# Triangular solve on one engine, one convolution tap and the update keys on others, and the diagonal blocks turned in one piece, in a gated delta-rule layer with experts

## The chip, the cores and the metric

One core of a Trainium2 chip runs the whole kernel as one program. It has five engines that run side by side, each with its own queue of instructions in a fixed order: PE (matrix products), DVE (vector), ACT (activations and copies), POOL (general elementwise work, indirect DMAs) and SP (DMA issues). They are kept in order by semaphores. The metric is device time in microseconds of one execution, median over runs.

## The reference

2048 tokens of width 256 pass two residual blocks in fp32. The first is a gated delta-rule layer with 8 key heads and 16 value heads of width 64; the second, 32 experts with 4 per token and a shared one.

```
qkv  = silu(causal_conv4(x @ W_qkv.T))          # depthwise, 4 taps, 2048 channels
q, k = l2norm(q) / 8, l2norm(k)                 # 8 heads, each used by two value heads
for t:                                          # per value head, state S is 64 x 64
    S     = S * exp(g_t)
    delta = (v_t - k_t @ S) * beta_t
    S     = S + outer(k_t, delta)
    o_t   = q_t @ S
y = rmsnorm(o) * norm_weight * silu(x @ W_z.T);   x = x + y @ W_out.T
x = x + moe(rmsnorm(layernorm(x))) + ...        # router, top 4, expert products, shared expert
```

## The kernel before, in words

The recurrence runs in chunks of C = 64 tokens (32 of them, `n`). Two chunks make a block of 128 tokens (`b`, 16), four make a pair (`p`, 8 pairs). Within a chunk the recurrence is a unit lower triangular system of 64 x 64 for each of the 16 heads, which is solved in advance for a whole pair: 4 chunks x 16 heads, split in diagonal blocks of H = 32 x 32, lie across the 128 partitions as 32 systems side by side.

One list, `SCHEDULE`, sets the order of all work. Each step has a due time in the tables `FRONT` (once for each pair), `CHAIN` (each chunk), `TAIL` (each block) and `GATE` (each pair); the list is sorted by due time, and every engine walks it and takes its own part of each step, in that order. The work of pair p+1's front stands between the chunks of pair p and the tails of its blocks. No step overtakes another in an engine's queue.

The steps that matter here, with their engines:

- `proj`, `mul`, `tap`, `silu`: the convolution, in 8 steps `s_` of two channel tiles `i`. PE projects 256 tokens and their halo into one of three PSUM banks in turn; ACT (line 600) copies it times the first tap to `ca` (two buffers, by `f % 2`); DVE (line 785) adds three taps from PSUM to it, 128x256 each; ACT (line 613) takes silu to `kqn` (steps 0 to 3, queries and keys) or `vraw` (4 to 7, values), and for queries and keys the squares (line 618). `ss`, `ssq`, `rpow` (POOL, line 477, a power) make the norms. A bank is free again after its last tap.
- `kt`, `kn`, `kb`, `ke`, `kk`, `nd`, `scan`, `nt`: keys by token (`ktok`) and normalised, decays by a scan (line 807), and the products (lines 818 and 819) to `ntx`, the triangular matrices, and `at`.
- `lx` (line 827): DVE turns the four diagonal blocks, 32 partitions each, to `nl`.
- `el`, j = 0 to 30: the forward elimination, a product with broadcast operands to a scratch tile (line 424) and a sum onto `tl` (line 427). Step j works on 31 - j rows; POOL takes columns 0 to 5, DVE columns 6 to j, each with a chain of its own. `xt` (lines 839, 840) turns the result; `pm`, `pe`, `tm`, `tc` make the lower left block of the inverse.
- For each chunk: `kqs` (POOL, line 519, two scalings), `ks`, `r`, `qs`, `sd` (POOL, line 527, scales the state), `u` (PE), then `up` (DVE, line 844), which scales u row by row by the decays to the end of the chunk, negated and times beta, into `rr`; `ue` (ACT, line 655) copies u to `us`; `ku` (PE, line 1147) multiplies keys and `rr`, two value heads of one key head at a time; `su` (DVE, line 849) adds to the state; `au`, `oe` give the output (ACT, line 661).
- For each block: `osq` (ACT, line 666), `nin`, `npow`, `yn` (DVE, line 868), `yt`, `yg` (DVE, line 874), `op` (PE, line 1187), `x2` (DVE, line 882), `xn`, `hh` and the router with its top 4 (`ex` on ACT, line 684; `tk`; `slot`, ending at line 931), `send` (POOL, line 546, four indirect DMAs). `z` and `zs` (PE, line 1171; ACT, line 671, silu) make the gates.

After the last pair come the experts, which the change doesn't touch.

## Time and profile before

| | us |
|---|---|
| median of 3 runs | 1326.2 (1325.64 to 1330.1) |
| the profiled execution | 1323.6 |
| its span | 1321.7 |
| busy: PE / DVE / ACT / POOL | 989.4 / 823.2 / 455.4 / 618.0 |
| mean granted clock of PE | 0.832 of full speed |

The profile is one execution; its span leaves out 1.9 us around the program. In a timeline each line begins with the start in us from the span's start and the duration in us; then engine, source line, operation, output and inputs, shapes, and the number of instructions. In brackets stands how long the engine was idle before and what ended that. Neighbouring instructions of an engine overlap a little, so that the distance from start to start is shorter than a duration. In a view by lines the columns behind the count are busy us, mean ns of one instruction and idle us before.

### The profile page before, as it was taken

The page shows a single profiled execution, that of the slowest core. Times are in us where ns is not written, and L with a number is a line of the kernel's source. Part 1 is how long each engine was busy: PE and PEld are TensorE (multiplying, and loading weights), DVE is VectorE, ACT ScalarE, POOL GpSimd, SP SyncE. Part 2 cuts the span into 40 slices and gives each one's busy share as a digit, 9 for nine tenths or more (in the row PEclk, how much of TensorE's full clock was granted, in tenths as well). Part 3 has the DMA queues.
Part 4 walks back from the last instruction along what each step waited for, and adds up shares of the span by engine and source line. Part 5 has one row for each costly group of instructions (what it writes and reads, how often), then busy time and mean ns, then how long its engine had stood idle before and what let it go on. Part 6 is the DMA issues. An engine that isn't in the chain of part 4 may idle for free.

```text
span 1321.7 us, 32155 instructions
## 1 busy us (share of the span) xinstructions
PE 989.4 (75%) x12359; PEld 810.8 (61%) x12359; DVE 823.2 (62%) x1947; ACT 455.4 (34%) x890; POOL 618.0 (47%) x907
## 2 busy tenths in 40 slices
PE   0673687787688879868787986878685799998950
PEld 0662675676577667657666765766675457776730
DVE  5169469569848956984895698489544243333335
ACT  1331422542253244225324422532422124444420
POOL 2036248447545744764484476448343013554530
PEclk9776789698778969877896987789588699999985
DMA  5270232505253360535336152533685922444437
GB/s 206 83 190 18 70 85 52 163 22 153 71 152 104 103 173 23 153 66 157 103 98 173 29 153 66 157 97 83 185 282 186 358 69 81 126 134 123 118 124 222
DMA packets 182356, 165.61 MB, mean 125 GB/s; under 512 B 75699, under 2 KB 174908, under 8 KB 181312
## 3 DMA queue, kind: packets, MB, share of 16 engines
q1 hardware_dynamic: 172272, 144.60, 38.9%
q0 software_dynamic: 7632, 16.87, 4.0%
q8 instruction: 102, 1.67, 0.5%
q10 hardware_dynamic: 2304, 2.10, 0.5%
q14 instruction: 46, 0.38, 0.1%
HBM read 66.03 MB, written 101.55 MB: 127 GB/s over the span
## 4 chain that ended last, share of the span: by engine, by line
PE 44%; DVE 34%; issue 9%; DMA 6%; ACT 4%; SPq 1%; POOL 1%; DVEq 0%; POOLq 0%; ACTq 0%
DVE arena L785 9%; PE ps L1039 5%; PE ps L1187 5%; PE ps L1249 5%; DVE arena L427 5%; DVE arena L424 4%; PE ps L1171 3%; PE ps L1102 3%; PE ps L1048 2%; PE ps L1092 2%; PE ps L1111 2%; PE ps L1272 2%; DMA out<-work 2%; PE ps L1156 2%; DMA work<-htd 2%
## 5 line engine op out<-in xcount | busy, mean ns | idle before, releaser
L785 DVE SCALAR_TENSOR_TENSOR arena<-ps,cw,arena 128x256 f32<-128x256 f32 x384 | 156.1, 475 | 84.2 <-ACT arena L600 83.1
L1039 PE MATMUL ps<-work,arena 128*128 128x259 f32 x512 | 162.6, 454 | 26.9 <-DVE arena L785 24.6
L557 POOL DMA_INDIRECT picked<-work x95 | 93.4, 983 | 111.4 <-DVE work L974 66.1
L1039 PEld LDWEIGHTS ps<-work,arena 128*128 128x128 f32 x512 | 107.4, 222 | 55.7 <-DVE arena L785 29.4
L600 ACT ACTIVATE arena<-ps,cw 128x256 f32<-128x256 f32 x128 | 60.2, 470 | 198.9 <-PE ps L1039 198.4
L546 POOL DMA_INDIRECT slotted<-hr,slots x64 | 63.3, 989 | 138.7 <-DVE slots L931 124.0
L964 DVE TENSOR_TENSOR work<-work,ps 128x128 f32<-128x128 f32 (+1 forms) x111 | 34.0, 307 | 140.6 <-ACT work L700 116.1
L477 POOL TENSOR_TENSOR rn<-rin,mhalf 128x16 f32<-128x16 f32 x16 | 46.5, 2906 | 153.7 <-DVE rin L791 153.7
L1249 PE MATMUL ps<-arena,work 128*128 x380 | 100.7, 387 | 7.4 <-issue 6.2
L427 POOL TENSOR_TENSOR arena<-arena 128x60 f32<-128x60 f32 (+29 forms) x248 | 92.1, 372 | 19.4
L424 POOL TENSOR_TENSOR arena<-arena 128x60 f32<-128x60 f32 (+29 forms) x248 | 89.4, 360 | 24.1 <-DVE arena L827 7.8
L1187 PE MATMUL ps<-work 128*128 128x256 f32 x256 | 73.9, 453 | 25.6 <-DVE work L874 25.6
L1171 PE MATMUL ps<-work 128*128 128x256 f32 x256 | 74.3, 440 | 18.8 <-DVE cnt L926 18.1
L427 DVE TENSOR_TENSOR arena<-arena 128x25 f32<-128x25 f32 (+12 forms) x200 | 81.2, 406 | 6.9
L1187 PEld LDWEIGHTS ps<-work 128*128 128x128 f32 x256 | 59.2, 235 | 40.4 <-DVE work L874 28.9
L613 ACT ACTIVATE arena<-arena 128x512 f32<-128x512 f32 x64 | 40.2, 629 | 123.2 <-DVE arena L785 123.2
L424 DVE TENSOR_TENSOR arena<-arena 128x25 f32<-128x25 f32 (+12 forms) x200 | 76.4, 382 | 4.3
L519 POOL TENSOR_TENSOR work<-arena,work 128x512 f32<-128x512 f32 x64 | 75.6, 1200 | 6.2 <-DMA work<-tab 6.0
L1249 PEld LDWEIGHTS ps<-arena,work 128*128 128x128 f32 x380 | 64.7, 190 | 18.9 <-issue 13.9
L700 ACT ACTIVATE work<-ps 128x128 f32<-128x128 f32 (+1 forms) x111 | 32.5, 292 | 120.8 <-PE ps L1240 56.9
L1171 PEld LDWEIGHTS ps<-work 128*128 128x128 f32 x256 | 52.3, 215 | 31.0 <-DVE cnt L926 18.9
L477 POOL TENSOR_TENSOR small<-small,mhalf 128x1 f32<-128x1 f32 x32 | 22.8, 713 | 97.9 <-DVE small L886 51.8
(221 smaller groups left out, 2234.7 us busy)
## 6 DMA issues: line engine op xcount, KB each, us to landing
slotted<-blank SPq DMA_DIRECT2D x17, 4128.0 KB
arena<-in_w SPq DMA_DIRECT2D x2, 6528.0 KB, 20.1
work<-slotted SPq DMA_DIRECT2D x95, 129.0 KB
arena<-tab SPq DMA_DIRECT2D x64, 128.0 KB, 3.5
work<-tab SPq DMA_DIRECT2D x64, 128.0 KB
...
```

Source lines behind the costliest of these rows:

```text
L424: e.tensor_tensor(t, nl[:, j + 1:H, j:j + 1].broadcast_to([P, rows, cols]), tl[:, j:j + 1, lo:hi].broadcast_to([P, rows, cols]), ALU.mult) ...
L427: e.tensor_tensor(tl[:, j + 1:H, lo:hi], tl[:, j + 1:H, lo:hi], t, ALU.add).then_inc(S[name], 1)
L477: g.tensor_tensor(out_, in_, mhalf[:, 0:in_.shape[1]], ALU.pow).then_inc(S[name], 1)
L519: g.tensor_tensor(kqs[:, n % 2, kind, :, :].rearrange("p (kt r) t -> p kt r t", r=2), kqn[:, p % 2, kind, :, lo:lo + C].unsqueeze(2).broad ...
L546: g.indirect_dma_start(out=slotted, out_offset=bass.IndirectOffsetOnAxis(ap=slots[:, k:k + 1], axis=0), in_=hr[:, k, :], in_offset=None).t ...
L557: g.indirect_dma_start(out=picked, out_offset=bass.IndirectOffsetOnAxis(ap=to, axis=0), in_=yrow[:, j % SLOTS, :], in_offset=None, bounds_ ...
L600: a.activation(ca[:, f % 2, i, :], bank_of("proj", p, s_, i)[:, 0:W2], ACT.Copy, scale=cw[:, u, 0:1]).then_inc(S["mul_out"], 1)
L785: v.scalar_tensor_tensor(out=acc_, in0=bank_of("proj", p, s_, i)[:, k:k + W2], scalar=cw[:, u, k:k + 1], in1=acc_, op0=ALU.mult, op1=ALU.a ...
L1039: ins = mm(to[:, 0:WX], wqkv[:, k, m:m + P], xt2[:, p % 3, k, :], start=k == 0, stop=k == KD - 1)
L1171: ins = mm(W3[:, W2 * j:W2 * j + W2], wz[:, d, m:m + P], xt2[:, p % 3, d, TAPS - 1:TAPS - 1 + W2], start=d == 0, stop=d == KD - 1)
L1187: ins = mm(W3[:, 0:DIM], ygt[:, u, :], wo[:, u, :], start=u == 0, stop=u == UT - 1)
L1249: ins = mm(up_[:, 0:2 * I], ht[:, j % 2, k, :], arena[:, bass.ds(at_ + 2 * I * k, 2 * I)], start=k == 0, stop=k == KD - 1)
```

## The change

Four edits and their new places in the order.

1. All columns of the elimination go to DVE, in one chain (62 instructions a pair instead of 50, on more elements); POOL's 62 small ones go.
2. The second tap is an ACT copy (scaled) into the place where silu's result will stand; DVE adds two taps; a new step `sum` on POOL adds the two 128x512 tiles; silu waits for it and its due time moves from 6.5 to 7.5.
3. `up` goes. A new POOL step `ktb` scales the keys instead, for each value head, ahead of the chunk; `ue` waits for u alone, and `ku` takes `ktb` and `us` in products of 64 columns, twice as many.
4. A new ACT step `lg` gathers the diagonal blocks with three copies into `xr`, and `lx` is one DVE transpose.

```diff
-SPLIT = 6
-ER = 2 * (H - 1 - SPLIT)
...
-         (24.5, "rpow", 1), (35, "lx"), (68, "xt"), (69, "tl"), (71, "pm"), (74, "pe"), (76, "tm"), (79, "tc")]
+         (24.5, "rpow", 1), (34.5, "lg"), (35, "lx"), (68, "xt"), (69, "tl"), (71, "pm"), (74, "pe"), (76, "tm"), (79, "tc")]
-          for t, what, *more in ((0, ("proj",), 0), (0.5, ("mul",), 0), (2, ("proj",), 1), (2.5, ("mul",), 1), (3.5, ("tap",)), (6.5, ("silu",)))]
-CHAIN = [(-14, "kqs"), (-13.9, "ebload"), (-4, "v"), (0, "ks"), (0.5, "qs"), (3, "r"), (4, "sd"), (4.5, "u"), (6.5, "up"), (7, "ue"),
+          for t, what, *more in ((0, ("proj",), 0), (0.5, ("mul",), 0), (2, ("proj",), 1), (2.5, ("mul",), 1), (3.5, ("tap",)), (6, ("sum",)), (7.5, ("silu",)))]
+CHAIN = [(-14, "kqs"), (-13.9, "ebload"), (-4, "v"), (0, "ks"), (0.5, "qs"), (3, "r"), (4, "sd"), (4.5, "u"), (-8, "ktb"), (6.5, "ue"),
...
     if name == "proj":
-        return [("tap", 6 * (8 * p + ix[0]) + 5 + ix[1])]
+        return [("tap", 4 * (8 * p + ix[0]) + 3 + ix[1])]
...
+        def conv_to(p, s_):
+            if s_ < 4:
+                return kqn[:, p % 2, s_ // 2, 2 * (s_ % 2):2 * (s_ % 2) + 2, :]
+            return vraw[:, p % 2, 2 * (s_ - 4):2 * (s_ - 3), :]
...
-                if name == "el":
...
-                    eliminate(pool, g, p, j, 0, min(SPLIT, j + 1), solve_tmp, "el_pool", EL * p + 2 * j)
+                if name == "sum":
+                    pool.wait_ge(S["tap"], 4 * f + 4)
+                    pool.wait_ge(S["mul_out"], 4 * f + 4)
+                    g.tensor_tensor(ca[:, f % 2, :, :], ca[:, f % 2, :, :], conv_to(p, s_), ALU.add).then_inc(S["sum_out"], 1)
+                if name == "ktb":
+                    pool.wait_ge(S["kn_out"], n // 2 + 1)
+                    pool.wait_ge(S["ndb_out"], 1)
+                    wait(pool, S["ku_mm"], n)
+                    g.tensor_tensor(ktb.rearrange("p (kt r) d -> p kt r d", r=2),
+                                    ktok[:, n // 2 % 4, n % 2, :, :].unsqueeze(2).broadcast_to([P, KT, 2, DH]),
+                                    ndb[:, n, :].rearrange("p (kt r) -> p kt r", r=2).unsqueeze(3).broadcast_to([P, KT, 2, DH]),
+                                    ALU.mult).then_inc(S["ktb_out"], 1)
...
+                    a.activation(ca[:, f % 2, i, :], from_[:, 0:W2], ACT.Copy, scale=cw[:, u, 0:1]).then_inc(S["mul_out"], 1)
+                    a.activation(conv_to(p, s_)[:, i, :], from_[:, 1:1 + W2], ACT.Copy, scale=cw[:, u, 1:2]).then_inc(S["mul_out"], 1)
                 if name == "silu":
-                    act.wait_ge(S["tap"], 6 * f + 6)
+                    act.wait_ge(S["sum_out"], f + 1)
+                if name == "lg":
+                    act.wait_ge(S["at_out"], 4 * p + 4)
+                    wait(act, S["pm_mm"], p)
+                    a.activation(xr, ntx[:, 0:H, :], ACT.Copy).then_inc(S["lg_out"], 1)
+                    act.wait_ge(S["lg_out"], 3 * p + 1)
+                    for e in range(2):
+                        own = slice(C * e + H, C * e + C)
+                        a.activation(xr[own], ntx[own, H:C, :], ACT.Copy).then_inc(S["lg_out"], 1)
                 if name == "r":
-                    wait(act, S["ku_mm"], n)
+                    wait(act, S["u_mm"], n)
                 if name == "ue":
-                    act.wait_ge(S["up_out"], n + 1)
+                    act.wait_ge(S["u_mm"], n + 1)
...
+            def eliminate(p, j):
+                rows, cols = H - 1 - j, j + 1
...
+                v.tensor_tensor(t, nl[:, j + 1:H, j:j + 1].broadcast_to([P, rows, cols]),
+                                tl[:, j:j + 1, 0:cols].broadcast_to([P, rows, cols]), ALU.mult).then_inc(S["el"], 1)
+                dve.wait_ge(S["el"], step + 1)
+                v.tensor_tensor(tl[:, j + 1:H, 0:cols], tl[:, j + 1:H, 0:cols], t, ALU.add).then_inc(S["el"], 1)
                 if name == "tap":
-                    dve.wait_ge(S["mul_out"], 2 * f + 2)
-                    for k in range(1, TAPS):
+                    for k in range(2, TAPS):
                         for i in range(2):
-                            if k > 1:
-                                dve.wait_ge(S["tap"], 6 * f + 2 * k - 3 + i)
+                            if k == 2:
+                                dve.wait_ge(S["mul_out"], 4 * f + 2 * i + 2)
+                            else:
+                                dve.wait_ge(S["tap"], 4 * f + i + 1)
                 if name == "lx":
-                    for q in range(4):
-                        rows, own = slice(H * q, H * q + H), slice(H * (q % 2), H * (q % 2) + H)
-                        v.transpose(nl[rows], ntx[rows, own, :]).then_inc(S["lx_out"], 1)
+                    dve.wait_ge(S["lg_out"], 3 * p + 3)
+                    v.transpose(nl, xr).then_inc(S["lx_out"], 1)
-                if name == "up":
-                    dve.wait_ge(S["u_mm"], n + 1)
-                    v.tensor_tensor(rr, by_head(UR), ndb[:, n, :].unsqueeze(2).broadcast_to([P, KR, DH]), ALU.mult).then_inc(S["up_out"], 1)
...
-                    pe.wait_ge(S["up_out"], n + 1)
+                    pe.wait_ge(S["ue_out"], n + 1)
+                    pe.wait_ge(S["ktb_out"], n + 1)
-                    for kt in range(KT):
+                    for h in range(KR):
                         for hp in range(2):
-                            ins = mm(KU[half(hp), P * kt:P * kt + P], ktok[half(hp), n // 2 % 4, n % 2, kt, :],
-                                     rr[half(hp), 2 * kt:2 * kt + 2, :].rearrange("p r d -> p (r d)"), start=True, stop=True)
+                            ins = mm(KU[half(hp), DH * h:DH * h + DH], ktb[half(hp), h, :], us[half(hp), h, :], start=True, stop=True)
```

By the new due times ACT's order in a pair reads (s for silu, m for the copies of a step and tile): m0,0 m0,1 r m1,0 m1,1 ue s0 m2,0 m2,1 s1 m3,0 oe m3,1 s2 s3 ke ke ht r ex ue lg oe osq zs m4,0 zs m4,1 zs zs r s4 ... ht r ex s7 ue pe oe osq tc. POOL's reads: sd sum0 kqs sum1 ktb rpow sum2 nd lnp sum3 nd rmp nd rpow nd sd kqs ktb send npow sum4 sd kqs sum5 ktb lnp sum6 rmp sd sum7 tl kqs ktb send npow. PE's is as before.

## Rows read from the trace of the kernel before

**Rows 1.** Stretches: us, busy PE, PEld, DVE, ACT, POOL, clock, DMA, GB/s

```profile
470.20:585.90 115.70, 92.97 (x1380) 78.44 (x1380) 86.32 (x205) 43.99 (x70) 65.02 (x96) 0.82 0.43 111
935.40:1015.40 80.00, 65.93 (x1048) 57.35 (x1048) 35.39 (x104) 27.60 (x41) 26.97 (x24) 0.78 0.72 224
1015.40:1321.70 306.30, 227.21 (x1057) 167.74 (x1056) 119.14 (x328) 96.57 (x326) 105.28 (x106) 0.88 0.51 157
```

**Rows 2.** Timelines of DVE, ACT and PE around the turns, pair 4

```profile
538.27 0.69 DVE L819 TENSOR_TENSOR arena<-ps,arena 128x512 f32<-128x512 f32 x1
...
539.92 5.04 DVE L827 STREAM_TRANSPOSE arena<-arena 32x1024 f32<-32x1024 f32 x4
...
548.49 2.44 DVE L785 SCALAR_TENSOR_TENSOR arena<-ps,cw,arena 128x256 f32<-128x256 f32 x6 [1.70 <-ACT arena L600]
...
535.94 1.28 ACT L671 ACT_TABLE_LOAD   x1
542.93 0.60 ACT L671 ACTIVATE work<-ps 128x512 f32<-128x512 f32 x1 [5.71 <-PE ps L1171]
...
545.07 2.00 PE L1171 MATMUL ps<-work 128*128 128x256 f32 x8
```

**Rows 3.** Timeline of DVE while it solves, pair 4

```profile
571.61 0.41 DVE L882 TENSOR_TENSOR row<-xin,ps 128x256 f32<-128x256 f32 x1
...
572.97 2.45 DVE L785 SCALAR_TENSOR_TENSOR arena<-ps,cw,arena 128x256 f32<-128x256 f32 x6
...
576.75 0.31 DVE L424 TENSOR_TENSOR arena<-arena 128x144 f32<-128x144 f32 x1
577.10 0.31 DVE L427 TENSOR_TENSOR arena<-arena 128x144 f32<-128x144 f32 x1
...
584.49 0.17 DVE L424 TENSOR_TENSOR arena<-arena 128x25 f32<-128x25 f32 x1
584.69 0.18 DVE L427 TENSOR_TENSOR arena<-arena 128x25 f32<-128x25 f32 x1
```

**Rows 4.** By lines, whole span: count, busy, mean ns, idle before

```profile
L519 POOL TENSOR_TENSOR work<-arena,work 128x512 f32<-128x512 f32 x64 | 75.6, 1200 | 6.2 <-DMA work<-tab 6.0
...
L600 ACT ACTIVATE arena<-ps,cw 128x256 f32<-128x256 f32 x128 | 60.2, 470 | 198.9 <-PE ps L1039 198.4
...
L844 DVE TENSOR_TENSOR work<-ps,ndb 128x512 f32<-128x512 f32 x32 | 21.8, 681 | 9.1 <-PE ps L1138 9.1
...
L666 ACT ACTIVATE work<-work 128x1024 f32<-128x1024 f32 x16 | 16.9, 1058 | 0.5
...
L839 DVE STREAM_TRANSPOSE arena<-arena 128x1024 f32<-128x1024 f32 x8 | 10.0, 1245 | 0.8
```

**Rows 5.** Timelines of DVE and POOL where both read SBUF

```profile
562.37 1.08 DVE L424 TENSOR_TENSOR arena<-arena 128x144 f32<-128x144 f32 x1
...
562.14 2.26 POOL L519 TENSOR_TENSOR work<-arena,work 128x512 f32<-128x512 f32 x2
...
551.62 1.23 DVE L868 TENSOR_TENSOR work<-work,nrm 128x1024 f32<-128x1024 f32 x1
...
551.63 1.53 POOL L424 TENSOR_TENSOR arena<-arena 128x135 f32<-128x135 f32 x1
...
933.10 1.08 DVE L424 TENSOR_TENSOR arena<-arena 128x25 f32<-128x25 f32 x1
```

**Rows 6.** Timelines of PE and POOL in the first steps, pair 4

```profile
503.67 2.03 PE L1048 MATMUL ps<-parind,arena 128*64 128x1 f32 x64 [0.66 <-ACT arena L618]
...
506.53 2.90 POOL L477 TENSOR_TENSOR rn<-rin,mhalf 128x16 f32<-128x16 f32 x1 [9.32 <-DVE rin L791]
```

**Rows 7.** Timeline of ACT behind the solve, pair 4

```profile
476.52 1.08 ACT L628 ACTIVATE arena<-ps 128x512 f32<-128x512 f32 x2 [2.32 <-PE ps L1092]
```

**Rows 8.** Timeline of DVE in pair 0, first and last of its solve

```profile
105.66 2.44 DVE L785 SCALAR_TENSOR_TENSOR arena<-ps,cw,arena 128x256 f32<-128x256 f32 x6
...
135.35 1.25 DVE L839 STREAM_TRANSPOSE arena<-arena 128x1024 f32<-128x1024 f32 x1
```

More of the change, by code:

```diff
@@ L184, in gated_delta_moe @@
         vraw = carve(2, UT, W2)
+        ktb = carve(KR, DH)
         parts = ((0, early), (early, EV))
@@ L416, in _ @@
                 sp.wait_ge(s_o[k], 16 * (NB // 2))
-        def eliminate(engine, e, p, j, lo, hi, scratch, name, step):
-            rows, cols = H - 1 - j, hi - lo
-            t = scratch[:, 0:rows * cols].rearrange("p (i k) -> p i k", i=rows)
-            if step % (2 * (H - 1 - lo)):
-                engine.wait_ge(S[name], step)
-            e.tensor_tensor(t, nl[:, j + 1:H, j:j + 1].broadcast_to([P, rows, cols]),
-                            tl[:, j:j + 1, lo:hi].broadcast_to([P, rows, cols]), ALU.mult).then_inc(S[name], 1)
-            engine.wait_ge(S[name], step + 1)
-            e.tensor_tensor(tl[:, j + 1:H, lo:hi], tl[:, j + 1:H, lo:hi], t, ALU.add).then_inc(S[name], 1)
         @block.gpsimd
@@ L616, in stage @@
                         wait(act, S["pm_mm"], p)
-                        wait(act, S["lx_out"], 4 * p)
+                        wait(act, S["lg_out"], 3 * p)
                         a.activation(sq[:, 2 * s_:2 * s_ + 2, :], dst, ACT.Square).then_inc(S["sqr_out"], 1)
+                if name == "lg":
+                    p, = ix
+                    act.wait_ge(S["at_out"], 4 * p + 4)
[5 more added lines that the diff above has]
+                        a.activation(xr[own], ntx[own, H:C, :], ACT.Copy).then_inc(S["lg_out"], 1)
                 if name == "ke":
@@ L773, in _ @@
             psum_, pinv, wsum, winv = (small[:, 15, k:k + 1] for k in range(4))
+            def eliminate(p, j):
+                rows, cols = H - 1 - j, j + 1
+                step = EL * p + 2 * j
+                t = solve_tmp[:, 0:rows * cols].rearrange("p (i k) -> p i k", i=rows)
+                if j == 0:
+                    dve.wait_ge(S["lx_out"], p + 1)
+                else:
+                    dve.wait_ge(S["el"], step)
+                v.tensor_tensor(t, nl[:, j + 1:H, j:j + 1].broadcast_to([P, rows, cols]),
+                                tl[:, j:j + 1, 0:cols].broadcast_to([P, rows, cols]), ALU.mult).then_inc(S["el"], 1)
+                dve.wait_ge(S["el"], step + 1)
+                v.tensor_tensor(tl[:, j + 1:H, 0:cols], tl[:, j + 1:H, 0:cols], t, ALU.add).then_inc(S["el"], 1)
             def stage(name, *ix):
@@ L797, in stage @@
                     dve.wait_ge(S["rn_out"], 2 * p + 1)
-                    wait(dve, S["ku_mm"], 2 * (b - 3))
+                    wait(dve, S["ktb_out"], 2 * (b - 3))
                     v.tensor_tensor(ktok[:, b % 4, :, :, :].rearrange("p e kt d -> p (e kt) d"),
```

43 lines of the change are left out of this document (17 added, 26 removed).

## The prediction

> **What bounds the kernel now.** I read the table of stretches first. Seven of the eight pairs repeat: the one from 470.2 to 585.9 takes 115.7 us, with DVE busy 86.3 us and PE 93.0, and the six others like it 115.8 to 117.4 [rows 1]. The span is a sum of such periods, with a head, an 80 us tail of the last chunks and 306 us of experts behind them [rows 1], which the change touches little or not at all. No engine is full over it, so I cut one pair (pair 4, 470.2 to 585.9) by what DVE waits for, in its own order of time. Four parts come out.
> A, 472.5 to 495.6: after the two turns of the solved blocks PE, ACT and the chunk's work run in line; DVE has long gaps.
> B, 495.6 to 516.7: four steps "projection, ACT copy, taps, silu"; PE and ACT set the pace.
> C and D, 516.7 to 550.9: scans and decay products on DVE until 539.0, then the four turns of the diagonal blocks (5.04 us), while ACT gates z; the taps of step 4 start at 548.49 after an idle gap for ACT's copies [rows 2].
> E, 550.85 (end of those taps) to 584.87 (end of the last elimination step, in front of the turns): DVE is back to back, 34.0 us, with no wait worth naming [rows 3]. It is the one part that DVE sets alone, and all of DVE's eliminations (from j = 6) lie in it.
> So DVE's share of a period, three quarters, says little: an instruction taken from DVE is worth its time in E and nearly nothing in A and B.
>
> **Solve on DVE, alone.** When POOL is idle a step on 25 elements takes 0.17 us and the next starts 0.20 later; one on 144 takes 0.31 and the next starts 0.35 later [rows 3]; two more of the kind give 0.34 and 0.33 for 144 and 133. That makes 0.17 us plus 1.18 ns per element from start to start. After the change step j works on (31-j)(j+1) elements, twice. Over j = 3 to 30 that is 56 instructions and 10,556 elements: 9.5 + 12.5 = 22.0 us. Steps 0 to 2 (6 instructions, 1.5 us) fall into the gap ahead of the taps of step 4, which DVE has today and keeps; if the gap were gone they would cost 1.5 us.
>
> **Taps, keys, turns.** Six taps of a step take 2.44 us, 0.39 from start to start [rows 2, 3]; four take 1.6. E holds three steps: 4.8 us instead of 7.2. The update scaling (L844, 0.68 us, 0.60 start to start [rows 4]) leaves DVE: one of the four in a pair lies in E, one in C, two in A or B beside waits. The rest of E stays: the normalisation 1.55, two gatings 1.2, the state 0.6, the residual and its statistics 1.35 (571.61 to 572.97 [rows 3]), the layer norm 0.65, the row h 0.8: 6.15 us. Uncontended E is thus 22.0 + 4.8 + 6.15 = 32.95 us, 1.1 less than now.
>
> **The lock.** DVE and POOL don't run at the same time when both read two SBUF tensors. While POOL's two key scalings ran (562.14, 2.26 us together), two DVE steps of 144 elements took 1.08 each (the first stands in the rows), against 0.31 alone: 0.77 lost apiece. The other way round, POOL's 135-element step that began with DVE's normalisation at 551.62 took 1.53 us [rows 5]. Taps read PSUM and one SBUF tensor and keep their 2.44 us beside POOL's steps [rows 2]. Today this costs E about 4.6 us: its 50 steps (5,850 elements) are worth 15.4 us alone by the formula and fill 34.0 - 7.2 - 0.6 - 6.15 = 20.0. The change takes POOL's small steps away, which pays that back, but puts large instructions in their place. In E stand four sums, one key scaling for the update (ktb), and, as before, two of kqs and one or two of sd, all 128x512 with two SBUF inputs, 1.04 us by themselves and 1.20 in the mean [rows 4]. A sum is released by the end of the taps, just when DVE goes back to the solve. Eight such instructions at 0.77 are 6.2 us. The bounds: 3 us, if half of them meet PSUM instructions or gaps, and 8.3 us, if each holds DVE for its 1.04. I take 0.77, the row that shows exactly this meeting. E becomes 32.95 + 6.2 = 39.1 us, 5.0 more than now.
> The Trainium skill (SBUF — State Buffer, section "Who interferes with whom") says that a Vector instruction with two SBUF inputs contends with a GpSimd instruction that reads SBUF and that the loser blocks for the whole of it. The rows above agree on who contends with whom; they show 0.77 us where the whole instruction would be 1.04, and by the page E would be 41.2 us instead of 39.1.
>
> **Turns and ACT (D).** Before: 5.04 us of turns from 539.92 [rows 2]. After: ACT gathers first, one copy of 128x1024 and two of 32x1024, each 1.06 us (as L666), in series some 3.2 us with the wait between them, then one turn of 1.25 (as L839) [rows 4]. The solve can begin 1.4 us sooner. But lg sits in ACT's queue ahead of oe, osq and the table load in front of the z gating: 3.2 (lg) + 0.6 + 1.06 + 1.28 from 539.0 puts the first gating at 545.1 instead of 542.93 [rows 2]. Behind it wait PE's second z product (545.07, now 545.8), the next projection and the copies of step 4, of which there are two more (0.47 us each [rows 4], start to start 0.4). The taps of step 4 then end at about 550.8, as now. D: 0, bounds -1.4 (zs not binding) and +1.5.
>
> **Steps 0 to 3 (B) and C.** Each step trades two taps (0.8 us) for two copies on ACT (0.4 on the path, the first pair hides behind PE) and a sum on POOL (1.04 us and a semaphore), so silu comes later by 0.8 us. In ACT's order silu 0 now stands behind mul 1,1 and ue, and silu 1 behind mul 2,1. Followed through, the squares of step 1 end at about 505.3, and the sum-of-squares product that stood at 503.67 [rows 6] starts 1.6 us later; through the output projection this reaches step 3. There the shorter taps give back 0.8. POOL's rpow (2.9 us at 506.53 [rows 6]) stands ahead of sum 2, and the sum ends near 512, before anything needs it. C loses 0.6 (one update scaling) and gains about 0.7 (ktb against DVE's top-k instructions). B and C together: +0.8, bounds -0.5 and +2.5.
>
> **A.** silu 7 moves behind ex, with its table load: 1.28 + 0.63 us more on ACT, which today sits idle 2.32 us before it copies the block products at 476.52 [rows 7]. So they fit, with 0.4 to spare, and the copy ue in the same gap is ready for the key update. POOL's row sends are untouched, ktb fits a POOL gap. The key update is 16 narrow products instead of 8 wide ones, which PE runs in about the same 1.1 us. A: 0, bounds -0.3 and +1.
>
> **Sum.** Pairs 1 to 7: +5.0 + 0.8 + 0 = +5.8 us each, 40.6. Pair 0 has no tails or kqs in its solve: today 29.7 us from 105.66 to 135.35 [rows 8]; after, 23.4 of steps, 6.4 of taps and 4 x 0.77 make 32.9 from about 105.0, 2.6 later, and 0.9 for its first four steps: 3.5. The tail of four chunks: 0 (an ACT copy of 0.59 in place of a DVE one of 0.68), bounds -1.5 and +1. Together +44.1 on a span of 1321.7, 1365.8. That execution took 1323.6 in all, so 1367.7, and the median of the runs lies 2.6 above it: **1370 us**. With the bounds of E (+1.8 to +7.1) and of B to D a period grows by 0 to 11 us.
>
> **Rivals.**
> 1. *The forecast*, 1352 to 1380, chance 0.54.
> 2. *The lock holds for the whole of a POOL instruction.* Each of eight takes 1.04 from DVE, +2.1 a pair, 1386. This is the Trainium skill's rule named above. The measured 0.77 speaks against it; for it, the 25-element step at 933.10, which met one of POOL's state scalings and took 1.08 us, 0.91 more than alone [rows 5]. Chance 0.12.
> 3. *POOL's order holds up silu.* Sum 2 and the others sit behind rpow, npow, kqs and row sends; if ss or the gating came another 3 us later in each pair through this, 1392 or more. It decides once a silu's lateness exceeds PE's work in between, about 3 us. Chance 0.08.
> 4. *The lock bites half as often*, since ktb, sd and kqs fall beside taps and PSUM reads: 3 us instead of 6.2, 1345. Chance 0.10.
> 5. *Faster: the relief of DVE reaches the end.* If the sums pass beside the solve without holding it (in the gaps between its short instructions, or because they start during the other DVE work), E is 33, 1.1 shorter; the earlier turn gives 1.4 if z's gating isn't what the taps wait for; the later silus are hidden. A period falls by up to 2.5, 1306 to 1318. It decides from a lock cost under 1 us per pair. For it: DVE's sum of work falls by 6.3 + 2.4 + 3.8 - 2.3 = 10.2 us per pair. Against it: the rows of the lock. Chance 0.12.
> 6. *It moves nothing*: losses in B and E meet the gain of D at zero. Chance 0.04.
>
> **How the numbers follow.** The time is that of case 1. The range 1322 to 1394 leaves out case 5 and the far end of case 3. Runs of this kernel differ by about 0.3%, so faster and slower count from there: faster 0.12, same 0.05, slower 0.83.
>
> **What would show it.** In the profile after: the stretch from the end of the taps of step 4 to the turn at 39 us (not 34); solve steps of 256 elements at 0.44 us but, next to each POOL sum, one of over 1 us; POOL sums of 1.0 to 1.2; DVE's taps down to 104 us in sum; lg's copies at 1.06 and the first z gating 2 us later against the last decay product; sum-of-squares of step 1 later by 1 to 2 us. It is wrong if periods are 116 us or less: then the lock was cheap, or the solve isn't on the path. It is wrong in size if gathering costs more than 3.2 us or steps with many elements take more than the line through 25 and 144 says.

## The result and the profile after

The change makes the kernel slower: 1399.4 us (median of 4, 1392.5 to 1400.7) beside 1328.2 us of the kernel before (median of 4 on the same chip), a ratio of 1.053 (95% interval 1.048 to 1.057). The forecast was 1370 us, the range 1322 to 1394. The sign was right; the loss is 71 us and not 42 to 44. The profiled execution has a span of 1398.8 us, 77.1 more than before.

The busy times stand in the page of the changed kernel:

```profile
PE 1023.8 (73%) x12871; PEld 844.4 (60%) x12871; DVE 809.2 (58%) x1859; ACT 526.0 (38%) x1044; POOL 549.5 (39%) x507
```

DVE is busy 14 us less than before and POOL 68 us less, and the kernel is 77 us longer: here the sums of busy time don't tell which way the time goes. I cut the pair with the same marks as before. The table of stretches of the changed kernel, with the columns of [rows 1], has for one pair the parts A (end of the turns to the end of the taps of step 0), B (to the end of the taps of step 3), C (to the last decay product), D (to the end of the taps of step 4) and E (to the end of the turns of the solved blocks):

```profile
633.20:659.30 26.10, 22.64 (x442) 19.90 (x444) 9.92 (x33) 16.61 (x23) 12.23 (x11) 0.65 0.76 195
659.30:681.20 21.90, 18.40 (x228) 15.52 (x226) 8.29 (x21) 8.50 (x18) 11.35 (x9) 0.84 0.08 19
681.20:704.60 23.40, 18.98 (x408) 17.77 (x404) 19.55 (x39) 6.47 (x11) 13.73 (x10) 0.81 0.30 87
704.60:716.60 12.00, 11.32 (x64) 8.82 (x66) 6.83 (x21) 9.22 (x13) 6.88 (x5) 0.79 1.04 276
716.60:759.50 42.90, 27.04 (x326) 21.56 (x322) 40.38 (x85) 11.67 (x24) 11.81 (x11) 0.82 0.20 48
```

| part, us | before | forecast of the change | after | change |
|---|---|---|---|---|
| A | 25.9 | 0 | 26.1 | +0.2 |
| B | 18.7 | B and C together +0.8 | 21.9 | +3.2 |
| C | 22.2 | | 23.4 | +1.2 |
| D | 12.0 | 0 | 12.0 | 0 |
| E, with 3.1 us of turns | 37.6 | +5.0 | 42.9 | +5.3 |
| period | 116.4 | +5.8 | 126.3 | +9.9 |

(means over pairs 2 to 7; they hardly vary after the change.) Pair 0 grew by 3.8 us, 3.5 was forecast. Pair 1 grew by 11.4 (100.7 to 112.1 us), as before the change its C and D were shorter than those of later pairs. At the end of the last pair's turns the changed kernel is 74.6 us behind, at the end of the program 77.1. So the totals of E, D, A and pair 0 came close to what was worked out. B and C did not, and the clock, the third number from the end of a row, is the first hint: 0.84 in B and 0.81 in C.

By lines (columns as in [rows 4]) the new and changed instructions are these, POOL's sum, DVE's taps, DVE's single turn:

```profile
L499 POOL TENSOR_TENSOR arena<-arena 128x512 f32<-128x512 f32 x64 | 82.5, 1289 | 228.6 <-DVE arena L809 228.6
...
L809 DVE SCALAR_TENSOR_TENSOR arena<-ps,cw,arena 128x256 f32<-128x256 f32 x256 | 109.9, 477 | 85.7 <-ACT arena L608 84.4
...
L849 DVE STREAM_TRANSPOSE arena<-arena 128x1024 f32<-128x1024 f32 x8 | 10.0, 1245 | 20.0 <-ACT arena L628 20.0
```

The sum takes 1.29 us, not the 1.04 to 1.20 of POOL's other instructions of that size.

Two detail views bear on the steps. **D**, ACT and DVE from the end of the last decay product at 704.6 on:

```profile
704.63 1.06 ACT L624 ACTIVATE arena<-arena 128x1024 f32<-128x1024 f32 x1 [8.12 <-DVE arena L843]
705.72 2.13 ACT L628 ACTIVATE arena<-arena 32x1024 f32<-32x1024 f32 x2
707.88 0.60 ACT L671 ACTIVATE work<-ps 128x512 f32<-128x512 f32 x1
709.58 1.28 ACT L681 ACT_TABLE_LOAD   x1
710.88 0.60 ACT L681 ACTIVATE work<-ps 128x512 f32<-128x512 f32 x1
...
707.88 1.25 DVE L849 STREAM_TRANSPOSE arena<-arena 128x1024 f32<-128x1024 f32 x1 [2.24 <-ACT arena L628]
```

The gather takes 3.2 us (704.63 to 707.85), the turn starts at 707.88 with 2.24 us of idle time before it, and behind gather, oe, squares and table load the first gating of z stands at 710.88, 6.3 us after the last decay product instead of 4.0 [rows 2]. What the single turn gives DVE, the gather in ACT's queue takes back, to 0.1 us.

**B**, ACT and PE of the same period:

```profile
661.19 0.47 ACT L607 ACTIVATE arena<-ps,cw 128x256 f32<-128x256 f32 x1 [1.98 <-PE ps L1055]
661.92 0.60 ACT L665 ACTIVATE work<-ps 128x512 f32<-128x512 f32 x1
665.23 0.47 ACT L607 ACTIVATE arena<-ps,cw 128x256 f32<-128x256 f32 x1 [0.80 <-PE ps L1055]
665.95 0.63 ACT L614 ACTIVATE arena<-arena 128x512 f32<-128x512 f32 x1
666.61 0.63 ACT L619 ACTIVATE arena<-arena 128x512 f32<-128x512 f32 x1
...
662.57 1.15 PE L1164 MATMUL ps<-work,arena 64*64 64x64 f32 x32 [0.54 <-ACT work L665]
667.39 2.62 PE L1064 MATMUL ps<-parind,arena 128*64 128x1 f32 x64 [2.20 <-DVE arena L809]
```

silu of step 1 (665.95) waits for the two copies of step 2 (665.23 and the one behind it), which wait for PE's projection, which is queued behind the key update (L1164, 662.57), which waits for ue (661.92), which is queued behind the copies of step 1 (661.19). The sum-of-squares product (L1064, 667.39) stands 34.2 us after the turns, instead of 31.2 [rows 6]; its row names DVE's taps as releaser, but those had long been done, and it starts 0.15 us after the squares of ACT (666.61 and 0.63).

### The profile page after: what moved, and what is told of

Same layout as the page of the kernel before. It is cut to its first block, busy times and chain, and to the rows that moved or that the text cites. A ratio compares the mean times of both kernels' runs of the same rounds, so it can differ in the third digit from the quotient of the medians.

```text
span 1398.8 us, 32933 instructions
## 1 busy us (share of the span) xinstructions
PE 1023.8 (73%) x12871; PEld 844.4 (60%) x12871; DVE 809.2 (58%) x1859; ACT 526.0 (38%) x1044; POOL 549.5 (39%) x507
## 3 DMA queue, kind: packets, MB, share of 16 engines
q1 hardware_dynamic: 172272, 144.60, 37.7%
## 4 chain that ended last, share of the span: by engine, by line
PE 46%; DVE 30%; issue 9%; DMA 7%; ACT 5%; POOL 2%; SPq 1%; DVEq 0%; POOLq 0%; ACTq 0%
DVE arena L796 7%; PE ps L1055 6%; PE ps L1203 6%; DVE arena L793 5%; DVE arena L809 4%; PE ps L1265 4%; PE ps L1118 3%; PE ps L1187 3%; PE ps L1064 3%; PE ps L1108 2%; PE ps L1172 2%; DMA out<-work 2%; PE ps L1127 2%; PE ps L1164 2%; PE ps L1256 2%
## 5 line engine op out<-in xcount | busy, mean ns | idle before, releaser
L1055 PE MATMUL ps<-work,arena 128*128 128x259 f32 x512 | 158.1, 444 | 24.5 <-DVE arena L809 21.7
L499 POOL TENSOR_TENSOR arena<-arena 128x512 f32<-128x512 f32 x64 | 82.5, 1289 | 228.6 <-DVE arena L809 228.6
L809 DVE SCALAR_TENSOR_TENSOR arena<-ps,cw,arena 128x256 f32<-128x256 f32 x256 | 109.9, 477 | 85.7 <-ACT arena L608 84.4
L607 ACT ACTIVATE arena<-ps,cw 128x256 f32<-128x256 f32 x128 | 60.3, 471 | 212.7 <-PE ps L1055 212.6
L796 DVE TENSOR_TENSOR arena<-arena 128x31 f32<-128x31 f32 (+15 forms) x248 | 127.6, 515 | 8.5
L793 DVE TENSOR_TENSOR arena<-arena 128x31 f32<-128x31 f32 (+15 forms) x248 | 101.0, 407 | 7.2 <-POOL arena L479 1.3
L1203 PE MATMUL ps<-work 128*128 128x256 f32 x256 | 84.3, 501 | 25.1 <-DVE work L890 25.1
L1187 PE MATMUL ps<-work 128*128 128x256 f32 x256 | 75.8, 446 | 27.3 <-DVE cnt L942 18.0
L1203 PEld LDWEIGHTS ps<-work 128*128 128x128 f32 x256 | 66.6, 265 | 42.9 <-DVE work L890 28.3
L471 POOL TENSOR_TENSOR small<-small,mhalf 128x1 f32<-128x1 f32 x32 | 22.9, 715 | 153.5 <-DVE small L902 118.7
L1187 PEld LDWEIGHTS ps<-work 128*128 128x128 f32 x256 | 53.3, 219 | 40.3 <-DVE cnt L942 18.8
L614 ACT ACTIVATE arena<-arena 128x512 f32<-128x512 f32 x64 | 40.4, 631 | 92.6 <-POOL arena L499 92.5
L521 POOL TENSOR_TENSOR work<-arena,work 128x512 f32<-128x512 f32 x64 | 70.3, 1118 | 7.4 <-DMA work<-tab 7.3
L608 ACT ACTIVATE arena<-ps,cw 128x256 f32<-128x256 f32 x128 | 60.1, 470 | 0.0
```

Source lines behind the costliest of these rows:

```text
L471: g.tensor_tensor(out_, in_, mhalf[:, 0:in_.shape[1]], ALU.pow).then_inc(S[name], 1)
L499: g.tensor_tensor(ca[:, f % 2, :, :], ca[:, f % 2, :, :], conv_to(p, s_), ALU.add).then_inc(S["sum_out"], 1)
L521: g.tensor_tensor(kqs[:, n % 2, kind, :, :].rearrange("p (kt r) t -> p kt r t", r=2), kqn[:, p % 2, kind, :, lo:lo + C].unsqueeze(2).broad ...
L793: v.tensor_tensor(t, nl[:, j + 1:H, j:j + 1].broadcast_to([P, rows, cols]), tl[:, j:j + 1, 0:cols].broadcast_to([P, rows, cols]), ALU.mult ...
L796: v.tensor_tensor(tl[:, j + 1:H, 0:cols], tl[:, j + 1:H, 0:cols], t, ALU.add).then_inc(S["el"], 1)
L809: v.scalar_tensor_tensor(out=acc_, in0=bank_of("proj", p, s_, i)[:, k:k + W2], scalar=cw[:, u, k:k + 1], in1=acc_, op0=ALU.mult, op1=ALU.a ...
```

## The experiments

All of them ran on other chips, on which the kernel before takes 1307 us instead of 1328. A ratio is always to runs of before on the same chip. The table gathers, from the traces, the parts of a period (means over pairs 2 to 7) beside the measured ratio.

| run | ratio (95% interval) | A | B | C | D | E | period |
|---|---|---|---|---|---|---|---|
| before_again | 1.000 (0.998 to 1.003) | 22.3 | 18.8 | 22.2 | 12.2 | 37.7 | 113.2 |
| solve_only | 1.018 (1.016 to 1.021) | 23.0 | 18.5 | 22.2 | 12.3 | 40.4 | 116.4 |
| tap_only | 1.011 (1.009 to 1.013) | 21.4 | 21.1 | 22.5 | 11.7 | 39.1 | 115.9 |
| keys_only | 1.004 (1.001 to 1.006) | 23.3 | 18.7 | 22.4 | 12.0 | 37.9 | 114.3 |
| turn_only | 1.004 (1.002 to 1.007) | 22.3 | 18.8 | 22.2 | 12.8 | 37.1 | 113.1 |
| tap_keys | 1.025 (1.020 to 1.030) | 22.7 | 21.2 | 22.6 | 11.4 | 39.6 | 117.5 |
| no_keys | 1.030 (1.027 to 1.033) | 21.7 | 20.3 | 22.2 | 12.0 | 42.4 | 118.5 |
| after_again | 1.041 (1.038 to 1.043) | 22.4 | 21.1 | 22.6 | 12.0 | 43.2 | 121.2 |
| act_order | 1.045 (1.042 to 1.048) | 22.5 | 21.3 | 22.7 | 12.0 | 42.6 | 121.2 |
| short_sums | 1.020 (1.017 to 1.023) | 22.4 | 21.9 | 22.7 | 12.0 | 38.2 | 117.3 |
| short_both | 1.018 (1.013 to 1.023) | 22.5 | 20.6 | 22.9 | 11.8 | 38.3 | 116.0 |
| slot_first | 0.993 (0.990 to 0.996) | 22.2 | 18.8 | 23.4 | 10.2 | 38.6 | 113.0 |

The spans behind the last pair differ between executions by up to 18 us (373.5 us in after_again, 391.6 in before_again). Of these 18, 8 lie in the last chunks, which the edits do touch, and 10 in the experts behind them, which no edit touches. So a difference of a period is read from the parts, and the ratio from the timed runs.

### Each edit alone

**solve_only.** The elimination as in the change, nothing else.

```diff
-                    eliminate(pool, g, p, j, 0, min(SPLIT, j + 1), solve_tmp, "el_pool", EL * p + 2 * j)
...
-                if name == "el" and ix[1] >= SPLIT:
+                if name == "el":
...
+                    eliminate(p, j)
```

> The kernel before with one edit of the four: all columns of the elimination on DVE, none on POOL. Theory 1 (the solve on DVE alone is the largest loss, by its own work): the stretch E of a pair, from the end of the taps of step 4 to the last elimination, is 22.0 of steps, 7.2 of taps, 0.6 of the update scaling, 6.15 of other work and three meetings with POOL's large instructions at 0.77, 38.3 us instead of 34.2. That is +4 us a pair and about 1358 us in all. Rival A (the loss of E is the lock between POOL's sums and DVE, and the solve alone would gain from a quiet POOL): E at 36 or less, 1342 or less. Rival B: the stretch is not what sets the time, 1326 to 1330.

Measured: 1333.0 us beside 1306.7. The stretch of E with its turns, one pair:

```profile
557.20:597.30 40.10, 25.11 (x282) 19.92 (x278) 38.31 (x92) 9.99 (x18) 5.51 (x6) 0.84 0.27 61
```

It takes 40.1 us, that is 37.0 without the turns, where 38.3 was expected and 36 or less by rival A: the solve by itself makes E 2.7 us longer in the mean. The trace says how. Against the line of the prediction (as a duration 0.14 us plus 1.18 ns per element) the steps of E take 5.6 to 6.0 us too long in the kernel before (pairs 3 to 5), not the 4.6 that I had worked out. Here the four large POOL instructions that are left, two key scalings and two state scalings, hold four steps for 3.1 us, and the other steps stand at the line. So DVE's own steps grow by some 6 us, the lock gives about 3 back, and the rest of E was taken about 2 us too long in the expected 38.3.

**tap_only.** ACT's second copy, POOL's sum, silu at 7.5, two DVE taps.

```diff
-                    for k in range(1, TAPS):
+                    for k in range(2, TAPS):
...
+                    g.tensor_tensor(ca[:, f % 2, :, :], ca[:, f % 2, :, :], conv_to(p, s_), ALU.add).then_inc(S["sum_out"], 1)
```

> The kernel before with one edit: the second tap as an ACT copy, summed by POOL, silu later in the order. Theory 2 (the first steps of a pair get longer because silu of step 1 waits behind the copies of step 2 on ACT and for POOL's sum): the taps of step 3 end 2 to 3 us later against the end of the solve before; in E POOL's own solve chain gets 4 sums of 1.2 to 1.3 us more, so E grows by 2 to 3 as well. Together +4 to +6 us a pair, 1355 to 1370 us. Rival: DVE's 0.8 us a step less in E comes through and the silus are hidden: 1315 to 1322.

Measured: 1322.1 beside 1306.7, that is 15.4 more, where the theory had 29 to 44 more (the expected times were written for a chip on which before takes 1326) and the rival 4 to 11 less. E grows by 1.4 us although DVE has 2.4 less of taps in it, and B by 2.3 while A gets 0.9 shorter (the first taps start before the second tile's copies are there) and D 0.5. The sign was right and the size about half. In E the cause is not the one expected: in pair 5 POOL's own solve chain ends at 701.47 us and DVE's at 703.91, so it is DVE that ends last, held by the sums (steps of 1.20 to 1.34 us).

**keys_only.** ktb in place of up.

```diff
-CHAIN = [(-14, "kqs"), (-13.9, "ebload"), (-4, "v"), (0, "ks"), (0.5, "qs"), (3, "r"), (4, "sd"), (4.5, "u"), (6.5, "up"), (7, "ue"),
+CHAIN = [(-14, "kqs"), (-13.9, "ebload"), (-4, "v"), (0, "ks"), (0.5, "qs"), (3, "r"), (4, "sd"), (4.5, "u"), (-8, "ktb"), (6.5, "ue"),
```

> The kernel before with one edit: update keys scaled by POOL ahead of the chunk, update scaling on DVE gone, 16 narrow products. Theory 2 (ue in ACT's order now stands between u and the key update): the key update of the first chunk of a pair comes 1 to 2 us later, and the sum of squares behind it; E loses 0.6 and gains a meeting with ktb at 0.77. +1 us a pair, about 1334 us. Rival: the shorter way from u to the key update shows, -0.6 us for each of 32 chunks on the path, 1310 to 1320.

Measured: 1311.3 beside 1306.7, +0.4%: the shorter way to the key update doesn't show, as B, C and E are within 0.2 us of before; A is 1.0 longer in this execution, which no step of mine explains.

**turn_only.** lg on ACT and one turn.

```diff
-                    for q in range(4):
-                        rows, own = slice(H * q, H * q + H), slice(H * (q % 2), H * (q % 2) + H)
-                        v.transpose(nl[rows], ntx[rows, own, :]).then_inc(S["lx_out"], 1)
+                    v.transpose(nl, xr).then_inc(S["lx_out"], 1)
```

> The kernel before with one edit: diagonal blocks gathered by three ACT copies and turned in one DVE instruction. Theory: the turn ends 1.5 us sooner, but the gating of z waits for the gather, so the taps of step 4 end where they did (12.0 us after the last decay product); the solve on POOL starts with the turn, so its part of E may end up to 1 us sooner. 1318 to 1328 us. Rival (ACT's gather is the new wait of the pair): later taps of step 4, +1.5 us a pair, 1338 us.

Measured: 1311.0 beside 1306.7. D is 0.6 longer and E 0.6 shorter. 3.8 us less of DVE's turns a pair gain nothing.

The four alone make +26.3, +15.4, +4.6 and +4.3 us, 50.6 in sum. The whole change, on a chip like theirs:

**after_again.** The changed kernel, no edit.

> The changed kernel once more, as the base for the runs beside it: 1.05 times the kernel before, a period of 126 us or the same less what this chip's part A takes less.

Measured: 1358.3 beside 1306.8, +51.5 us. The sum of the four and the whole agree. But the ratio is 1.041 here and was 1.053 on the chip of the first measurement (intervals apart): the same edits cost 20 us less here than the 71 there.

### The lock

**short_sums.** The changed kernel with the sum on 16 of 256 columns of each tile; the rest of the sum is left out, so the result is no longer that of the reference.

```diff
-                    g.tensor_tensor(ca[:, f % 2, :, :], ca[:, f % 2, :, :], conv_to(p, s_), ALU.add).then_inc(S["sum_out"], 1)
+                    g.tensor_tensor(ca[:, f % 2, :, 0:16], ca[:, f % 2, :, 0:16], conv_to(p, s_)[:, :, 0:16], ALU.add).then_inc(S["sum_out"], 1)
```

> The changed kernel with POOL's sum on 16 of 256 columns of each tile; the rest of the second tap is left out of the convolution. Same instructions in the same order, POOL's sum about 0.25 us instead of 1.29. Theory 1 with the lock: four sums in E give back 0.77 each, so E is 36.8 instead of 39.9, and B and C together are 0.5 to 1.5 shorter: 26 to 35 us less than the changed kernel. Rival (the lock is a minor part, DVE's own steps are the loss): E above 38.9, under 10 us less.

Measured: 1331.5 us, 26.8 less than after_again. Its B and E of one pair:

```profile
382.50:404.40 21.90, 18.39 (x228) 15.61 (x226) 8.30 (x22) 8.50 (x18) 8.34 (x9) 0.84 0.15 36
438.80:477.10 38.30, 26.22 (x328) 20.95 (x324) 36.48 (x86) 11.87 (x24) 7.89 (x11) 0.86 0.24 60
```

E is 38.3 us in this pair and 38.2 in the mean (35.1 without the turns; 36.8 was expected), where it is 43.2 in after_again and 42.9 in the changed kernel of the first measurement: 4.7 to 5.0 us for four sums. B is 21.9 at a clock of 0.84, as in after_again at the same clock, so the length of POOL's sum is not what makes B long. In the changed kernel the meeting looks like this, DVE and below it POOL, right behind the taps of step 4:

```profile
716.49 0.27 DVE L793 TENSOR_TENSOR arena<-arena 128x112 f32<-128x112 f32 x1
716.79 1.26 DVE L796 TENSOR_TENSOR arena<-arena 128x112 f32<-128x112 f32 x1
718.08 0.30 DVE L793 TENSOR_TENSOR arena<-arena 128x135 f32<-128x135 f32 x1
718.42 1.09 DVE L796 TENSOR_TENSOR arena<-arena 128x135 f32<-128x135 f32 x1
...
716.65 1.27 POOL L499 TENSOR_TENSOR arena<-arena 128x512 f32<-128x512 f32 x1 [2.31 <-DVE arena L809]
718.31 1.04 POOL L529 TENSOR_TENSOR work<-work,ec 128x512 f32<-128x512 f32 x1 [0.39 <-PE ps L1144]
```

A step of 112 elements takes 0.27 us ahead of the sum and 1.26 beside it, 0.99 more. The next meeting, with POOL's state scaling of 1.04 us, makes 1.09 of 0.30 for 135 elements, 0.79 more: the 0.77 of my forecast. Now the ends: DVE's step starts 0.14 us into the sum and ends 0.13 after it (718.05 and 717.92); the other starts 0.11 into the scaling and ends 0.16 after it (719.51 and 719.35). Both times DVE stood until POOL's instruction was through. This is the rule of the Trainium skill (SBUF — State Buffer, section "Who interferes with whom"): the loser blocks for the whole instruction, and the trace agrees. The 0.77 that I held against it is the rule's own result, 1.04 less DVE's late start and less the part of the step (0.30 less 0.16) that is its own run anyway. What was wrong was the length put in, not the lock.

The whole of E can be counted in this way. The steps of DVE that are far above the line are these, besides the first four (1.26 us at 716.79 and 1.09 each at 718.42, 719.54 and 720.66), and one wait:

```profile
730.45 1.37 DVE L796 TENSOR_TENSOR arena<-arena 128x247 f32<-128x247 f32 x1
731.85 1.14 DVE L793 TENSOR_TENSOR arena<-arena 128x252 f32<-128x252 f32 x1
...
741.36 0.42 DVE L898 TENSOR_TENSOR row<-xin,ps 128x256 f32<-128x256 f32 x1 [0.64 <-PE ps L1203]
...
744.70 1.34 DVE L796 TENSOR_TENSOR arena<-arena 128x220 f32<-128x220 f32 x1
...
749.66 1.19 DVE L793 TENSOR_TENSOR arena<-arena 128x135 f32<-128x135 f32 x1
...
755.19 1.26 DVE L796 TENSOR_TENSOR arena<-arena 128x31 f32<-128x31 f32 x1
```

Nine steps are held, for 7.9 us together. The four sums (716.79, 730.45, 744.70, 755.19) hold them for 0.94 to 1.08 us each, 3.9 in all; the other five (two key scalings, two state scalings, one `ktb`) for 0.70 to 0.89 each, 3.9 in all. In short_sums the five remain, 4.0 us, and the four are gone. The rest of the 4.7 to 5.0 us is the wait for PE's output projection ahead of the residual (L898): 0.64 us here, 0.92 and 1.01 in two pairs of after_again, none in short_sums.

### The first steps

**act_order.** The changed kernel with two due times changed.

```diff
-          for t, what, *more in ((0, ("proj",), 0), (0.5, ("mul",), 0), (2, ("proj",), 1), (2.5, ("mul",), 1), (3.5, ("tap",)), (6, ("sum",)), (7.5, ("silu",)))]
+          for t, what, *more in ((0, ("proj",), 0), (0.5, ("mul",), 0), (2, ("proj",), 1), (2.5, ("mul",), 1), (3.5, ("tap",)), (6, ("sum",)), (6.4, ("silu",)))]
...
-CHAIN = [... (-8, "ktb"), (6.5, "ue"), ...
+CHAIN = [... (-8, "ktb"), (6.4, "ue"), ...
```

> The changed kernel with two due times changed: silu at 6.4 instead of 7.5, ue at 6.4 instead of 6.5, so that on ACT silu of step 1 stands ahead of the last copies of step 2 and ue ahead of the last copies of step 1. Theory 2 (the order on ACT carries the loss of B): the sum-of-squares product of a pair comes 1.3 to 2 us sooner, the taps of step 3 too; 9 to 15 us less than the changed kernel. Rival (B is long because of POOL's sum and the doubled copies, wherever silu stands): within 4 us of the changed kernel.

Measured: 1363.7 us, 5.3 more than after_again, and B is 21.3 instead of 21.1: this order gains nothing, as the rival said. With silu ahead, ACT waits for the sum in silu's place and the copies behind it are late. But the edit moved more than theory 2 asked for: silu of step 0 also went ahead of ue and of the last copies of step 1, and these copies start 26.7 us after the turns instead of 24.9 (a pair of each). So the run shows that this order is no better, not that ACT's order has no part in B; an order with silu of step 1 alone moved was not run.

**short_both.** The changed kernel with the second copy and the sum both on 16 columns, the rest of both left out.

```diff
-                    a.activation(conv_to(p, s_)[:, i, :], from_[:, 1:1 + W2], ACT.Copy, scale=cw[:, u, 1:2]).then_inc(S["mul_out"], 1)
+                    a.activation(conv_to(p, s_)[:, i, 0:16], from_[:, 1:17], ACT.Copy, scale=cw[:, u, 1:2]).then_inc(S["mul_out"], 1)
```

> The changed kernel with the second ACT copy and POOL's sum on 16 of 256 columns; the rest of the second tap is left out of the convolution. With POOL's sum alone cut, B stayed at 21.9 us at a clock of 0.84. Theory 4 (the second copies on ACT make B longer): 0.3 us a copy, up to four of them in line before the sum of squares, B is 1 us shorter at the same clock, D 0.3 to 0.6 shorter, so 8 to 12 us less than with the sum alone cut (1331 us). Rival (B is long by PE's clock and the key update): within 3 us of it.

Measured: 1326.7 us, 4.8 less than with the sum alone cut, with intervals that overlap. B is 19.8 or 21.4 in single pairs, by the clock, where short_sums has 21.9: at 0.84 the copies are worth 0.5 us. Theory 4 had 1 us: they are a part of B, and a small one.

**tap_keys.** The two edits that meet on ACT, those of tap_only and keys_only together, on the kernel before.

> The kernel before with two edits, the tap and the update keys. Theory 3 (together they cost more than the 1.1% and 0.4% each costs alone, because ue stands behind the doubled copies): 1.025 times the kernel before, 1340 us. Rival (they add): 1.015 times, 1326 us.

Measured: 1337.2 us, 1.025 (1.020 to 1.030) as theory 3 said, where the two alone make 1.015.

**no_keys.** The changed kernel without the keys edit: its `up` and its wide key update are those of before.

```diff
-CHAIN = [... (4.5, "u"), (-8, "ktb"), (6.5, "ue"), ...
+CHAIN = [... (4.5, "u"), (6.5, "up"), (7, "ue"), ...
...
-                            ins = mm(KU[half(hp), DH * h:DH * h + DH], ktb[half(hp), h, :], us[half(hp), h, :], start=True, stop=True)
+                            ins = mm(KU[half(hp), P * kt:P * kt + P], ktok[half(hp), n // 2 % 4, n % 2, kt, :],
```

> The changed kernel without the edit of the update keys (three edits of four). Theory 3 (the edits cost more together than alone: with the doubled copies in front of it, ue on ACT makes the key update late, which the keys edit alone didn't show): B shortens by 2 us or more, C by 0.7, E by 0.2: 18 to 25 us less than the changed kernel. Rival (the edits add up): 5 us less, as that edit cost alone.

Measured: 1345.1 us, 13.2 less than after_again. The tap and the keys together cost 30.2 us (tap_keys, its interval 27 to 39) where they cost 20.0 apart, and the keys 13.2 in the whole where they cost 4.6 alone: 9 to 10 us more together. The chain shown in B above gives one place: ue, which the key update now waits for, stands behind doubled copies. It is not the whole of it. At a like clock B is 19.6 and 21.2 us without the keys edit (no_keys, pairs 2 and 3) and 19.9 and 21.9 with it (after_again), 0.3 to 0.7 a pair or 2 to 5 us over seven pairs, and the mean B of tap_keys is that of tap_only. The rest isn't placed. The sum of the four still meets the whole because solve and turn, 30.6 us alone, add only 21.3 to tap_keys; where those 9 us go I didn't trace. My expectation of 18 to 25 for the keys was too high.

**before_again.** The kernel before, for its trace.

> The kernel before, for its trace beside the ones of this chip. E 34.2 us and the stretch B (end of the taps of step 0 to the end of those of step 3) 18.7 us where PE is granted 0.91 of full speed, as before; if the clock of B is 0.84 in some pairs, as in the changed kernel's runs, then B is 20 us or more in those and not in the others (theory: the clock sizes B), or 18.7 in all (rival: it doesn't).

One pair, parts A to E:

```profile
467.40:489.40 22.00, 21.72 (x438) 19.47 (x439) 11.12 (x36) 15.06 (x19) 13.57 (x12) 0.70 0.80 226
489.40:508.20 18.80, 16.03 (x196) 13.11 (x196) 11.03 (x29) 6.69 (x14) 5.47 (x4) 0.91 0.11 28
508.20:530.40 22.20, 15.95 (x390) 14.76 (x384) 18.67 (x39) 9.40 (x14) 11.08 (x7) 0.96 0.21 63
530.40:542.50 12.10, 11.99 (x90) 9.59 (x92) 9.93 (x20) 2.74 (x5) 9.08 (x13) 0.80 1.09 293
542.50:580.10 37.60, 25.00 (x284) 19.85 (x278) 35.81 (x87) 10.04 (x18) 25.69 (x61) 0.86 0.29 65
```

B is 18.8 us at 0.91 in every pair, so this run alone can't tell what the clock does. Others can. turn_only has B's instructions of before unchanged, and its B fell on three clocks (the third number from the end is the granted clock):

```profile
264.10:281.20 17.10, 14.32 (x194) 11.85 (x194) 10.94 (x28) 6.69 (x13) 5.47 (x4) 1.00 0.11 27
375.40:395.70 20.30, 17.53 (x194) 14.36 (x194) 10.95 (x28) 6.69 (x13) 5.61 (x5) 0.83 0.10 27
490.10:508.90 18.80, 16.03 (x194) 13.07 (x194) 10.99 (x29) 6.69 (x13) 5.47 (x4) 0.91 0.11 27
```

17.1 us at 1.00, 18.8 at 0.91, 20.3 at 0.83: 3.2 us between the ends, with the same work. PE's busy time grows by the same 3.2 (14.32, 16.03, 17.53), and the rest of B stays at 2.8 us. So the share of B at the lower level (1.2 GHz) sets its length. (One pair of solve_only has 17.2 us at 0.90; there DVE came 1.6 us late to the taps of step 0, where B begins, and A with B is as long as elsewhere, 41.8 and 41.5.) after_again shows the same for the changed kernel, B and then C:

```profile
397.80:417.70 19.90, 16.39 (x214) 13.65 (x214) 8.34 (x22) 8.50 (x18) 11.34 (x9) 0.91 0.14 35
519.00:540.90 21.90, 18.40 (x229) 15.66 (x226) 8.31 (x22) 8.49 (x18) 11.33 (x9) 0.84 0.08 20
417.70:441.10 23.40, 18.97 (x408) 17.77 (x402) 19.55 (x39) 6.47 (x11) 13.73 (x10) 0.81 0.26 78
540.90:563.40 22.50, 16.07 (x408) 14.88 (x403) 19.60 (x39) 6.36 (x11) 14.36 (x10) 0.97 0.24 70
```

B takes 19.9 us at 0.91 and 21.9 at 0.84, and what isn't PE's busy time is 3.5 us in both. C takes 22.5 at 0.97 and 23.4 at 0.81. The changed kernel of the first measurement had 0.84 and 0.81 in every pair from 2 to 7, the kernel before 0.91 in B. Beside before_again, with 0.91 in B and 0.96 in C, B grew by 1.1 us and C by 0.3 at the clock of before; the other 2.1 and 0.9 us came with the clock. For C this holds in the changed kernel only. The first trace of the kernel before has C at two clocks, and it is 22.2 us at both:

```profile
516.80:539.00 22.20, 17.55 (x390) 16.36 (x384) 18.68 (x39) 9.40 (x14) 11.07 (x7) 0.87 0.21 61
632.70:654.90 22.20, 15.95 (x390) 14.76 (x384) 18.68 (x39) 9.40 (x14) 11.07 (x7) 0.95 0.21 64
```

PE's 1.6 us more of busy time are hidden there; in the changed kernel, with 2.9 us more at 0.81, 0.9 come through.

### A version that is a little faster than both

**slot_first.** The kernel before with one due time changed.

```diff
-        (33.5, "base"), (35.5, "tk"), (38.5, "rank"), (40, "slot"), (42, "send"), (43, "blanks")]
+        (33.5, "base"), (35.5, "tk"), (38.5, "rank"), (38.4, "slot"), (42, "send"), (43, "blanks")]
```

> The kernel before with one due time changed: slot at 38.4 instead of 40, so that DVE frees PE's bank for the z products before the last decay products of the pair and not behind them. D, in which DVE waits for the copies of step 4, should shrink by 1.2 to 1.4 us, since PE waits 2.98 us for slot there: 8 to 11 us less than before, 1296 to 1299 us. Rival (the wait moves to the taps of another step or to PE's order): within 3 us of before.

Measured: 1295.9 us beside 1306.9, 0.993 (0.990 to 0.996), faster than both kernels. The time is what was expected and the reason isn't shown: D shrank by 2.0 us, more than expected, but C grew by 1.2 and E by 0.9, so the period is only 0.2 shorter in the profile. The profiled execution took 1306.0 us, the slowest of its ten, and so doesn't hold the gain that the median shows; where the 11 us come from stays open.

## Why the prediction was right and wrong

- **What bounds the pair: right.** E is set by DVE but for one wait for PE of 0.6 to 1.0 us, and the other parts by PE and ACT. Taking 3.8 us a pair from DVE in D gave nothing (turn_only); more solve work on DVE in E gave +1.8%, locks and all (solve_only).
- **The solve and the formula: right.** The line of 0.17 us and 1.18 ns per element holds: the 46 steps of E that aren't held take together 3% less than it says. Worked out for E: 39.1 us; measured 39.8 (42.9 less 3.1 of turns). That the two are so close is in part luck: without lock and wait E is 31.3 (39.8 less 7.9 and 0.6), and I had 32.95.
- **The lock: right in kind, the term mis-sized.** 0.77 for each of eight, 6.2 us, was taken; the trace has nine held steps and 7.9 us. The four sums cost 0.94 to 1.08 each, because a sum takes 1.26 to 1.37 us and not 1.04; the five others cost 0.70 to 0.89, as forecast. This term is 1.7 too low and the uncontended work 1.65 too high: the two errors cancel. That the sum would take as long as the key scaling was an assumption from its size; the row of its own kind didn't exist.
- **The turn and the gather (D): right**, to 0.1 us in the end of the taps, by the chain that was given.
- **Steps 0 to 3 and C: the step that failed.** It said +0.8 and measured +4.4. Of this, 1.4 are there at an unchanged clock, so the working was short by 0.6: I followed the sum-of-squares product to 1.6 us late and it was 3.0 late. The key update behind ue came 2.2 us later, and the projection of step 2's second tile stands behind it on PE; my working has neither. The other 3 us a period, some 18 of the 33 us that the forecast of the span lacks, are PE at its lower level in B and C. I took durations of PE from one execution and let them stand when the gaps between them changed; the prediction has no term for the clock, and its bound for B and C, +2.5, was therefore too narrow.
- **A: right in the difference (+0.2).** Its level differs between chips, 25.9 on the first and 22.3 on the others for the kernel before.
- **Pair 0: right**, 3.8 for 3.5. **Pair 1** was counted like the later ones, at +5.8; it grew by 11.4. **The tail** grew by 2.5 where 0 was forecast with an upper bound of 1; executions differ there by more than that.
- **The rivals.** Number 2, the whole-instruction lock, is what the rows show, and its 8.3 us for the lock are nearer to the measured 7.9 than my 6.2. It would have given 1386 and is still not the reason for the missing 29 us: E came out 0.7 longer than I forecast, not 2.1, as the work beside the lock was less. Number 3, POOL's order, is not what happened: in pairs 2 to 7 seven of the eight sums start 0.08 us after their last tap. Only that of step 2 stands behind `rpow`, 5.8 us, and it ends at 674.4 in pair 5, long before its silu, which stands behind the copies of step 3 until 679.8. Number 4, half the lock, falls with the count of 7.9 us, number 5, faster, with solve_only, and number 6, no change, with the ratio.

What stays open is why PE's clock in B and C is lower in every pair of the changed kernel on the first chip and in half of them on another. The runs show that B's length goes with the clock, not what it takes to lose it. No run changed the clock by itself.
